# Input's group norm in three lots of images, the second block's weights turned into other banks, convolution set 0 in two halves by row group

## The reference

```python
def _gn(v, G=32, eps=1e-05):      # per image, per group of 4 channels
    ...
x = x + L0(_gn(x))   # L0: chan_ln -> 1x1 q,k,v -> depthwise 3x3 each -> softmax, linear attention
                     #     -> silu -> 1x1 -> chan_ln
x = x + L1(_gn(x))   # L1: 1x1 qkv -> depthwise 5x5 -> grouped 1x1 -> relu attention on both
                     #     -> 1x1 -> batch norm (constants)
return x
```

## Time and profile before

| | |
|---|---|
| three timed runs | 282.09, 285.93, 286.94 us (median 285.93) |
| the profiled execution | 284.52 us, of which the span shown in the trace is 282.8 us |
| PE busy | 245.7 us (87% of the span) |
| DVE busy | 189.6 us (67%) |
| ACT busy | 156.5 us (55%) |
| POOL busy | 112.3 us (40%) |

### The profile page before, as it was taken

How to read it: one execution, slowest core, us unless ns; L and a number is a source line. 1 busy time by engine, 2 the same in 40 slices (tenths; PEclk the granted TensorE clock), 3 DMA queues, 4 the chain that set the end, 5 groups by cost and what they waited for, 6 DMA issues and landing times. The chain is left out here.

```text
span 282.8 us, 12240 instructions
## 1 busy us (share of the span) xinstructions
PE 245.7 (87%) x5253; PEld 187.4 (66%) x5253; DVE 189.6 (67%) x542; ACT 156.5 (55%) x381; POOL 112.3 (40%) x215
## 2 busy tenths in 40 slices
PE   0369999788999899996988989989899999689994
PEld 0255666576686687775666777667679998466661
DVE  5683787658996478998858556630205988767873
ACT  1268695779954578785583076423453347822320
POOL 8384435458694556735531353101121221443100
PEclk9999999999999999999999999999999999999999
DMA  7711288492001100000091905761454400002222
GB/s 216 173 36 23 53 203 198 111 205 64 3 5 31 47 3 2 0 3 2 3 207 21 221 24 117 177 144 57 111 151 141 132 22 6 0 3 77 77 74 74
DMA packets 18309, 22.77 MB, mean 81 GB/s; under 512 B 4416, under 2 KB 10560, under 8 KB 18256
## 3 DMA queue, kind: packets, MB, share of 16 engines
q1 hardware_dynamic: 16576, 21.42, 30.5%
q10 hardware_dynamic: 1680, 0.58, 1.0%
HBM read 5.64 MB, written 4.29 MB: 35 GB/s over the span
## 5 line engine op out<-in xcount | busy, mean ns | idle before, releaser
L1205 PE MATMUL bank<-cin,tband 64*32 64x240 f32 (+5 forms) x2632 | 83.4, 397 | 3.5 <-issue 2.8
L1205 PEld LDWEIGHTS bank<-cin,tband 64*32 64x32 f32 x2632 | 67.1, 106 | 18.3 <-issue 8.2
L687 ACT ACTIVATE tband<-tband,row_edge 128x96 f32<-128x96 f32 (+1 forms) x96 | 31.9, 396 | 22.3 <-POOL tband L517 21.4
L961 DVE STREAM_TRANSPOSE cin<-bank 128x768 f32<-128x768 f32 x32 | 31.1, 977 | 16.2 <-PE bank L1205 15.9
L1201 PE MATMUL bank<-ident,rings 128*128 128x128 f32 x192 | 32.1, 294 | 7.4 <-DVE rings L1108 2.4
L1201 PEld LDWEIGHTS bank<-ident,rings 128*128 128x128 f32 x192 | 22.8, 149 | 21.1 <-issue 10.7
L1013 DVE STREAM_TRANSPOSE cpos<-bank 64x256 f32<-64x256 f32 x56 | 25.1, 447 | 16.8 <-PE bank L1205 16.1
L568 POOL TENSOR_SCALAR ring_v<-cpos,mask_b 128x512 f32<-128x512 f32 x30 | 20.8, 708 | 33.3 <-PE bank L1205 18.8
L517 POOL TENSOR_TENSOR tband<-taps,pw 128x160 f32<-128x160 f32 x24 | 10.7, 460 | 44.1 <-PE bank L1205 44.1
L637 ACT ACTIVATE rings<-bank,ln_b,ln_s 128x128 f32<-128x128 f32 x64 | 24.1, 461 | 6.4 <-POOL ln_b L488 6.3
L1205 PE MATMUL bank<-w0t,rings 128*32 128x192 f32 x512 | 24.4, 337 | 0.7 <-ACT rings L660 0.7
(11 more groups left out here) (128 smaller groups left out, 419.8 us busy)
## 6 DMA issues: line engine op xcount, KB each, us to landing
cin<-cin SPq DMA_DIRECT2D x32, 192.0 KB, 3.9
cin<-cin SPq DMA_DIRECT2D x34, 128.0 KB, 2.8
xin<-in_x_dram SPq DMA_DIRECT2D x4, 512.0 KB, 6.2
q_rows<-rings SPq DMA_DIRECT2D x16, 128.0 KB
out_dram<-rings SPq DMA_DIRECT2D x16, 128.0 KB, 1.7
cin<-cin SPq DMA_DIRECT2D x16, 64.0 KB, 2.0
cpos<-q_rows SPq DMA_DIRECT2D x4, 256.0 KB
cpos<-q_rows SPq DMA_DIRECT2D x8, 128.0 KB
```

The source lines that it names most:

```text
L687: last = a.activation(dst[:, :, 1 + e], dst[:, :, 0], ACT.Copy, scale=row_edge[:, e:e + 1])
L961: v.transpose(cin[:, :, 2 * n, i // 2, :, o:o + QN // 2], ps[:, :, 0:UC].rearrange("p l (s c) -> p s l c", c=CG)).then_inc(s_cin, 1)
L1205: return t_.matmul(dst, stationary, moving, start=start, stop=stop, skip_group_check=True)
```

## The change

It has three parts. First, input's group norm is done in three lots (images 0 to 3, 4 to 7, 8 to 15) with sums in banks 5, 6 and 7; PE, DVE, ACT and POOL each get their steps at new places, block 0's weights are turned into bank 4 and copied by ACT behind the second pair's scaled images, and on POOL `tap_rows` moves from behind lot 0's scale to behind the last lot's. Second, the second block's weights go to banks 2 and 3 instead of 4 and 5, and PE no longer waits for `s_cin` ahead of them. Third, convolution set 0 is done in two halves: all tap rows for column groups 0 and 2 first, then the wait for the odd quads, then column groups 1 and 3. The diff, without lines that only renumber lots:

```diff
+GN0 = ((0, 4), (4, 8), (8, 16))
+NL0 = len(GN0)
...
+        def gn_sums0(c):
+
+            return bank[5 + c]
...
(POOL)
-            gn_scale(0, 0, B // 2)
-            tap_rows()
+            gn_scale(0, GN0[0][0], GN0[0][1] - GN0[0][0])
+            gn_scale(1, GN0[1][0], GN0[1][1] - GN0[1][0])
             for i in range(PAIRS):
                 layernorm(i)
                 if i == 1:
-                    gn_scale(1, B // 2, B // 2)
+                    gn_scale(2, GN0[2][0], GN0[2][1] - GN0[2][0])
+                    tap_rows()
...
(ACT)
-            act.wait_ge(s_wt, 1)
-            act.wait_ge(s_w0, 16 * 5)
-            a.activation(w0t[:, :], bank[0][:, 0:3 * C], ACT.Copy, scale=vecs[:, 0:1])
-            a.mul(owt[:, :], bank[0][:, 3 * C:4 * C], 0.5).then_inc(s_wte, 1)
...
             act.wait_ge(s_gn, 1)
             xg(0)
-            for step in range(PAIRS + 2):
+            xg(1)
+            act.wait_ge(s_wt, 1)
+            act.wait_ge(s_w0, 16 * 5)
+            a.activation(w0t[:, :], bank[4][:, 0:3 * C], ACT.Copy, scale=vecs[:, 0:1])
+            a.mul(owt[:, :], bank[4][:, 3 * C:4 * C], 0.5).then_inc(s_wte, 1)
+            for step in range(1, PAIRS + 2):
...
                 if step == 1:
+                    act.wait_ge(s_gn, 2)
                     xg(2)
...
-                    if step + 1 == PAIRS // 2:
-                        act.wait_ge(s_gn, 2)
+                    if step + 1 == GN0[2][0] // 2:
+                        act.wait_ge(s_gn, 3)
...
-                   bank[4][:, 0:3 * C].rearrange("p (h t e) -> p h t e", t=3, e=HD1))
+                   bank[2][:, 0:3 * C].rearrange("p (h t e) -> p h t e", t=3, e=HD1))
...
(DVE)
-            link(x_stats(0, B // 2))
-            gn_aggregate(0, 0, B // 2)
-            gn_variance(0, 0, B // 2, bank[7])
-            gn_read(0, B // 2, bank[7])
-            x_stats(B // 2, B - 4)
+            link(x_stats(0, 4))
+            gn_aggregate(0, 0, 4)
+            x_stats(4, 7)
+            gn_variance(0, 0, 4, gn_sums0(0))
+            link(x_stats(7, 8))
+            gn_aggregate(1, 4, 4)
+            gn_read(0, 4, gn_sums0(0))
+            x_stats(8, 11)
             dve.wait_ge(s_gn, 1)
...
-            link(x_stats(B - 4, B))
-            gn_aggregate(1, B // 2, B // 2)
+            gn_variance(1, 4, 4, gn_sums0(1))
+            x_stats(11, 12)
+            gn_read(1, 4, gn_sums0(1))
             for step in range(PAIRS + 3):
+                if step == 3:
+                    gn_read(2, 8, gn_sums0(2))
...
                 if step < PAIRS:
                     moments(step, bank[X_BANKS[step % 3]][:, :])
-                if step == 0:
-                    gn_variance(1, B // 2, B // 2, bank[7])
                 if step == 1:
-                    gn_read(1, B // 2, bank[7])
-
+                    link(x_stats(12, 16))
+                    gn_aggregate(2, 8, 8)
+                if step == 2:
+                    gn_variance(2, 8, 8, gn_sums0(2))
...
(PE)
             for k in range(2):
-                gn_mean(0, k, 0, B // 2, bank[7])
-
+                gn_mean(0, k, 0, 4, gn_sums0(0))
+
+            gn_mean(1, 0, 4, 4, gn_sums0(1))
             pe.wait_ge(s_ident, 1)
             pe.wait_ge(s_w0, 16 * 5)
             for n in range(4):
-                last = t_.transpose(tile(bank[0], n), wst[n], ident[:, :])
+                last = t_.transpose(tile(bank[4], n), wst[n], ident[:, :])
             last.then_inc(s_wt, 1)
-            pe.wait_ge(s_wte, 1)
...
-                    if i == 0 and n == 1:
-                        pe.wait_ge(s_gnr, 2)
+                    if i == 0:
+                        pe.wait_ge(s_gnr, NL0 if n else 2)
+                        pe.wait_ge(s_wte, 1)
                     units(n, ring_c[:, i % 2, :], w0t, 4).then_inc(s_qkv, 1)
+                    if i == 0 and n == 0:
+                        gn_mean(2, 1, 8, 8, gn_sums0(2))
                     if n == 0 and i + 1 < PAIRS:
                         back(i + 1)
...
             xg_transpose(0)
-            gn_mean(1, 0, B // 2, B // 2, bank[7])
+            gn_mean(1, 1, 4, 4, gn_sums0(1))
             xg_transpose(1)
             xg_transpose(2)
-            gn_mean(1, 1, B // 2, B // 2, bank[7])
+            gn_mean(2, 0, 8, 8, gn_sums0(2))
             back(0)
...
-            pe.wait_ge(s_cin, 2 * PAIRS)
             for n in range(3):
-                t_.transpose(tile(bank[4], n), wst[4 + n], ident[:, :])
+                t_.transpose(tile(bank[2], n), wst[4 + n], ident[:, :])
             for n in range(3):
 
-                last = product(tile(bank[5], n), pwrep[:, n].rearrange("p x c -> p (x c)"), ident[:, :])
+                last = product(tile(bank[3], n), pwrep[:, n].rearrange("p x c -> p (x c)"), ident[:, :])
...
                 if n == 0:
-                    pe.wait_ge(s_da, (XQ - 1) * 16 * 8)
-                    pe.wait_ge(s_odd, 4 + 2 + 4)
-                    pe.wait_ge(s_oddp, 4 + 2)
+                    pe.wait_ge(s_cin, 2 * PAIRS)
...
-                for k in order:
-                    dy = k - ks // 2
-                    lo, hi = max(0, -dy), min(HH, HH - dy)
-                    for j in (0, 2, 1, 3):
+                for js in ((0, 2), (1, 3)) if n == 0 else ((0, 2, 1, 3),):
+                    if n == 0 and js[0] == 1:
+                        pe.wait_ge(s_da, (XQ - 1) * 16 * 8)
+                        pe.wait_ge(s_odd, 4 + 2 + 4)
+                        pe.wait_ge(s_oddp, 4 + 2)
+                    for k, j in itertools.product(order, js):
+                        dy = k - ks // 2
+                        lo, hi = max(0, -dy), min(HH, HH - dy)
```

More of the change, by code:

```diff
@@ L18 @@
+import itertools
 from contextlib import ExitStack
@@ L574, in gn_of_lot @@
                 i0, i1, _ = GN1[c]
-                gn_scale(2 + c, 2 * i0, 2 * (i1 - i0))
+                gn_scale(NL0 + c, 2 * i0, 2 * (i1 - i0))
             pool.wait_ge(s_ce, NS)
@@ L703, in _ @@
             a.copy(w1t[:, :].rearrange("p (t h e) -> p h t e", t=3, e=HD1),
-                   bank[4][:, 0:3 * C].rearrange("p (h t e) -> p h t e", t=3, e=HD1))
+                   bank[2][:, 0:3 * C].rearrange("p (h t e) -> p h t e", t=3, e=HD1))
             a.copy(w1q[:, :].rearrange("p (g s e) -> p g s e", g=2, e=HD1),
-                   bank[4][:, 0:3 * C].rearrange("p (s g t e) -> p g s t e", g=2, t=3, e=HD1)[:, :, :, 0])
+                   bank[2][:, 0:3 * C].rearrange("p (s g t e) -> p g s t e", g=2, t=3, e=HD1)[:, :, :, 0])
             for g in range(2):
                 last = a.copy(pw[half(g), :, :].rearrange("p (t s) o -> p t s o", t=3),
-                                  bank[5][half(g), 0:3 * C].rearrange("p (s g t o) -> p g t s o", s=TS, g=2, t=3)[:, g])
+                                  bank[3][half(g), 0:3 * C].rearrange("p (s g t o) -> p g t s o", s=TS, g=2, t=3)[:, g])
             last.then_inc(s_wte, 1)
@@ L768, in xg1 @@
             def xg1(i):
-                act.wait_ge(s_gn, 3 + [i < i1 for i0, i1, _ in GN1].index(True))
+                act.wait_ge(s_gn, NL0 + 1 + [i < i1 for i0, i1, _ in GN1].index(True))
                 if i < 2:
@@ L1080, in x1_stats @@
                         link(last)
-                        gn_aggregate(2 + c, 2 * i0, 2 * (i1 - i0))
+                        gn_aggregate(NL0 + c, 2 * i0, 2 * (i1 - i0))
             def kv_mask(n):
@@ L1115, in gn_variance_of_lot @@
                 i0, i1, _ = GN1[c]
-                gn_variance(2 + c, 2 * i0, 2 * (i1 - i0), gn_sums[c])
+                gn_variance(NL0 + c, 2 * i0, 2 * (i1 - i0), gn_sums[c])
             def gn_read_of_lot(c):
                 i0, i1, _ = GN1[c]
-                gn_read(2 + c, 2 * (i1 - i0), gn_sums[c])
+                gn_read(NL0 + c, 2 * (i1 - i0), gn_sums[c])
             for step in range(FRONT1 + PAIRS + 1):
@@ L1427, in raw_q @@
             def raw_q(i):
-                pe.wait_ge(s_q1, i) if i else pe.wait_ge(s_gnr, 4)
+                pe.wait_ge(s_q1, i) if i else pe.wait_ge(s_gnr, NL0 + 2)
                 product(bank[4][:, :], w1q[:, :], xg_slot(i)).then_inc(s_qp, 1)
@@ L1476, in o_transpose @@
                 if n == 0:
-                    pe.wait_ge(s_gnr, 5)
+                    pe.wait_ge(s_gnr, NL0 + 3)
                 else:
@@ L1485, in gn_of_block1 @@
                     pe.wait_ge((s_ke, s_sl, s_x1)[c], PAIRS)
-                gn_mean(2 + c, k, 2 * i0, 2 * (i1 - i0), gn_sums[c])
+                gn_mean(NL0 + c, k, 2 * i0, 2 * (i1 - i0), gn_sums[c])
             for step in range(FRONT1 + PAIRS + 2):
```

## The result

| | before | changed |
|---|---|---|
| timed beside each other | 285.5 us (4 runs) | 287.0 us (4 runs) |
| again, with ten runs of the changed kernel | 285.3 us | 288.9 us |
| the profiled execution, and its span | 284.52 us, 282.8 | 285.93 us, 284.2 |

The ratio is 1.0109 with an interval of 1.0059 to 1.0159, and 1.0084 (1.0046 to 1.0121) the second time: slower by 2.4 to 3.1 us, within 2%. The ratios leave out executions in a slower state of the chip, which the medians include. The prediction was 288.0 us and no change of 2%. The total came out as forecast; the parts did not all do so. The traced execution of the changed kernel was the fastest of its four.

A forecast was written before the change was run, and what follows sets the result against it. PE was taken as the bound, busy 18.00 of 18.00 us from 30 to 48 us. +3.5 at the third pair and -0.7 at set 0 give +2.8 on 285.2: 288.0 us, range 285.2 to 290.5.

The forecast's parts named there:

- The first lot: Start of block 0: with statistics of four images first, the scale is there at 11.05, 2.45 us earlier.
- What eats it again: Chain from first scaled image to first unit: of 2.45 us gained, 1.25 are left; `back(0)` at 19.5, unit at 21.3.
- The step that turns the sign: POOL, third pair: last scale and `tap_rows` delay the layer norm; PE idles about 4.3 us, `back(2)` 3.5 us late.
- What PE does after standing idle: Behind the third pair's stall: slow PE work could cost up to +1.8 us; the forecast took nothing.
- rival 1: Units behind PE's stall start slow: +2.8 + 1.8 = +4.6, 289.8 us; chance 0.28.
- Rivals 3 and 4: 3: third layer norm isn't late, 283.7 us, chance 0.05; 4: smaller stall by fast first unit, 287.1 us, chance 0.15.
- The turn: From block 0's units to its convolution: early weight turns and half of set 0 within the copy wait, -0.7 us.
- The half that comes off the path: Convolution set 0: its first half ends within the wait for ACT's copies, taking 0.70 us off.
- Sum: Whole kernel: +3.5 at the third pair, nothing made up, -0.7 at set 0: +2.8 us, 288.0 us.
- rival 2: Convolutions' waits by issue, 2.8 us, close after PE's stall and set 0's early start: 285.2 us; chance 0.12.

The follow-up runs named there:

- the kernel that stays busy: Changed kernel, but PE does the second pair's first unit three times over to keep working: 284.5 us, ratio 0.9977.
- the experiments on POOL's order and the slow unit: Changed kernel with tap copies ahead of the last scale: 284.2 us; changed kernel with PE doing the second pair's first unit three times: 284.5 us.

## Why the prediction was right or wrong

**The first lot: right.** ACT's first scaled image was forecast for 11.05 and starts at 10.79.

**What eats it again: right in kind, 0.7 us too dear.** `back(0)` was to start at 19.5 and starts at 18.79, the first unit at 20.56 instead of 21.3. Each step of the chain was a little early, so that the third lot's first products start at 17.92 and not at 18.6. It made no difference: this unit took 2.79 us where the earlier trace rows have 2.40, and the third lot's scale starts on POOL at 24.16; 24.3 was forecast.

**The step that turns the sign: right.** Scale done at 26.1 (forecast 26.3), copies at 28.6 (28.95), layer norm at 30.57 (30.8), `back(2)` at 32.22 (32.4): 3.31 us late, not 3.5. PE's idle time is 3.59 and not 4.3, since slow units kept it busy until 28.63. The runs with POOL reordered confirm the cause, and that nothing is made up afterwards in block 0's front.

**What PE does after standing idle: wrong.** "I take nothing, the nearer to rows" was the choice that failed. The transposition and unit behind the gap took 0.39 and 1.22 us more, 1.6 us in all (2.3 in the second trace), around the upper bound of 1.8 that the text gave, and the slow PE of rival 1 is what happened, though not its total of 289.8 us. (Rivals 3 and 4 did not: the third layer norm was late, the first unit slow.) The rows taken as nearer, gaps of up to 1.2 us, are at most a third of this one; in the kernel that stays busy the granted clock stayed at 1.00 behind 1.67 us of idle time, and here it read 0.56 to 0.58 behind 3.59.

**The turn: right place, wrong size.** "The half that comes off the path is 0.70" took half the products for half the time. The half set's 24 records lasted 1.45 us, 60 ns each, as long as the forecast gave the whole set at 29 ns each, and the second half takes 1.57 us up to DVE's read where the whole set takes 1.64. A half set has as many products per column group as a whole one, on two groups instead of four; the times fit products of one group that follow each other while the groups run side by side. In the traces 0.2 us came off.

**Sum.** Forecast for DVE's first read: 3.5 - 0.7 = 2.8 us late. Measured: 3.3 for the stall, 1.6 for the slow unit, 0.2 off for the halves, and 0.2 for one gap between later units, ahead of the transposition at 46.14 us: 4.88. Then 1.5 came back in the convolution and 1.7 from its end up to the output's first products (154.87 us before, 153.13 after), of which these rows are the two ends, before and changed:

```profile
87.93 0.66 PE L1201 MATMUL bank<-ident,cpos 128*128 128x128 f32 x4
242.80 1.13 PE L1205 MATMUL bank<-xin,wpt 128*128 128x512 f32 x2
...
91.27 0.66 PE L1216 MATMUL bank<-ident,cpos 128*128 128x128 f32 x4
244.40 1.12 PE L1220 MATMUL bank<-xin,wpt 128*128 128x512 f32 x2
```

With 0.2 behind that, 1.4 is left for the span. The prediction had none of the last three. Its own rival 2 named the waits by issue, but as something that a stalled PE closes; the table shows waits of any size with and without a stall. The kernel before can also lose time late: in its second trace it spent 42.06 us behind those output products, not 40.00, at a lower clock. So the medians, 1.5 and 3.6 us apart, agree with 2.8 because a term left out and a gain left out nearly cancel, which is luck: a right total with one wrong term of +1.6, another of +0.5, and some 2 us by the ratios (3.5 in the traced execution) given back that were not foreseen and are not fully explained.

## What to carry to other kernels

When a step is moved on an engine that works in order, write down what stands behind it and when each input of that was ready: a layer norm whose moments were there at 19.05 waited until 28.72 behind a scale that had to wait for PE and behind copies, and the whole cure was to put it ahead of them. Price a stall of several microseconds on PE twice, once as idle time and once as slow work behind it. And half of a set of products that run side by side need not be half of its time (1.57 us against 1.64 here): count the products that follow each other in one column group.

## What the runs showed of the hardware that was not expected

- The longest gap alone doesn't tell whether the granted clock falls. In the kernel before, waits of 1.56, 0.71 and 1.10 us around 243 to 250 us went by at a granted clock of 1.00; its second execution had 1.61, 0.71 and 0.66 there, and fell to 0.50; with the banks alone it fell to 0.51 in the same place. Gaps of 1.67 and 1.85 us in the experiments on POOL's order and the slow unit went by at 1.00. Stretches of the second execution of the kernel before (columns as above):

```profile
244.00:248.00 4.00, 2.22 (x40) 2.04 (x40) 1.51 (x4) 1.73 (x5) 2.88 (x4) 0.87 0.02 4
248.00:252.00 4.00, 3.34 (x42) 2.82 (x42) 1.98 (x6) 0.71 (x2) 1.37 (x2) 0.50 0.00 0
```

- At the start the column reads 1.00 although the first unit takes 2.79 us, nearly the 2.73 us at 33 us, where it reads 0.58 and 0.56. The durations suggest the lower level at the start too; the column doesn't show it.
- PE's convolution products waited between 0.2 and 3.7 us by issue, by up to 2.3 us differently in two executions of one program. A gain of 1 us cannot be read from one trace of this kernel's span; it can from the distance of two rows with a known cause between them, as the 1.68 and 1.89 us here.
